# Cross attention of a decoder's first layer: waits for each PSUM bank on its own, and the shifted products of four banks issued obliquely

## The chip, the cores and the metric

The kernel runs on one core of a Trainium2 chip. TensorE (PE) multiplies matrices into eight banks of PSUM, VectorE (DVE) and ScalarE (ACT) read the banks, SyncE (SP) issues transfers. The engines run side by side and meet at semaphores only. The metric is the device time of one launch in microseconds (us), median over runs; lower is better.

## What is computed

The program is a decoder of four layers (attention, cross attention and a feed forward block each) on 16 sequences of 128 tokens of width 256. The change touches layer 0's cross attention alone:

```python
def _L0_xattn_ref(hidden_states, attention_mask, adapter, Wq, Wk, Wv, Wo, gate):
    ...                                   # 32 heads of width 8, rotary tables cos and sin
    scores = jnp.einsum('bhqd,bhkd->bhqk', q, k) * inv_sqrt_d + attention_mask
    w = jax.nn.softmax(scores)            # the row maximum is taken off before exp
    attn_output = jnp.einsum('bhqk,bhkd->bhqd', w, v)
    a_scores = jnp.einsum('bhqd,bhkd->bhqk', q, a_k) * inv_sqrt_d
    a_scores = jnp.tanh(gate) * jax.nn.softmax(a_scores)
    attn_output = attn_output + jnp.einsum('bhqk,bhkd->bhqd', a_scores, a_v)
    return attn_output @ Wo
x = x + _L0_xattn_ref(_layernorm(x), mask, ctx_2048, ...)
```

So each sequence has 64 attention matrices of 128 x 128: 32 of the tokens with themselves (with the mask) and 32 with the context (without it).

## The kernel before

`L0_xattn` is a software pipeline over the 16 sequences (batches). `ring_of_three` runs turns b = -2 to 16, those from 1 to 12 in a loop whose body holds three turns. In turn b, batch b gets its exponentials and its output, batch b+1 ("ahead") its scores and row maxima, batch b+2 ("entering") its projections, and batch b-1 ("behind") its last part. Every engine has its own instruction list in a fixed order, and waits in it on counting semaphores.

`QuadRows` makes the attention of one batch in four rounds i = 0 to 3 (s, c = divmod(i, 2)): rounds 0 and 1 are attention with itself (s = 0), 2 and 3 with the context (s = 1). A round has 16 heads: row group r (four groups of 32 partitions) times slot j (four key sets `kM`, in each of which all heads but one are zero). The four groups write four banks, `work_bank` = banks 2 to 5, called banks 0 to 3 here by their r. The same four banks are used in turn by two kinds of work:

- `scores_tensor` (batch b+1): in rounds 0 and 1 first `mask_tensor`, 16 small products of an identity block with the mask (32 x 32 tiles of the array, 512 columns), then one product per bank (L972, 512 columns). DVE then takes the row maxima of bank after bank (`maxima_vector`, L1037) and counts `top_found` for each.
- `shifts_tensor` (batch b): the mask again in rounds 0 and 1, then per bank four products in the transposed direction (L985, slot j, 128 columns, float32) and four that add the negated maxima (L990, bfloat16). With the last of a bank PE counts `shifted`. ACT takes the exponentials of bank after bank (`exp_scalar`, L1022) and counts `p_ready` for each.

`mix_tensor` (L1003) multiplies the exponentials of a round with v. PE's order in a full turn is: scores(0), a transpose and projections, mix(3) of batch b-1, shifts(0), scores(1), mix(0), shifts(1), projections with wk and wkr (L199), scores(2), mix(1), projection with wo (L208), shifts(2), a transpose of `raw` (L191), projections with wq and wqr, scores(3), mix(2), transposes, shifts(3), projections with wv (L208), a transpose of `raw`. DVE's order is: maxima(0), the layer norm, normalize, maxima(1), split, rotate k (L1329 to L1331), maxima(2), spread keys (L1336), the residual (L888), normalize, rotate q (L1329 to L1331), maxima(3), normalize, split, normalize.

What frees a bank is told by `score_free` and `shift_free`: a score needs the exponentials (`p_ready`) of the round before, a shift needs the maxima (`top_found`) of the scores of the same round. Both take the bank's number r, and the kernel before calls them once a round, with the last bank (`PAIRS` has one group of four and `some[-1]` is 3).

## Time and the profile before

| | |
|---|---|
| median of 3 runs | 4075.38 us (4067.34 to 4081.88) |
| profiled execution, its own time | 4076.79 us |
| its span, first to last instruction | 4075.0 us |
| PE busy over the span | 3285.3 us (81%) |
| DVE / ACT busy | 2605.6 us (64%) / 1758.6 us (43%) |
| granted PE clock, mean | 0.903 |
| L0 cross attention, where the change is | about 140 us to 745 us of the span |
| in 140 to 750 us: PE, DVE, ACT busy | 484.88, 320.30, 243.32 us of 610 |

The whole kernel is a row of such phases with a barrier behind each, so time saved in this one is saved as a whole, and what lies behind it only moves. A row of the timeline gives start, duration over all merged instructions, engine, line, operation and, in brackets, how long the engine had been idle before and what released it. In this program each float32 matmul of the source (transposes apart) is two MATMUL records, a bfloat16 one is one. The ends of matmuls are modelled, so a matmul row ends a little after the next may begin.

### The profile page before, as it was taken

How to read it: one execution, taken by the hardware profiler on the slowest of the kernel's cores; microseconds unless marked ns; L12 is line 12 of the kernel's file. 1: busy time of each engine (PE TensorE's matmuls, PEld its weight loads, DVE VectorE, ACT ScalarE, POOL GpSimd, SP SyncE). 2: the span in 40 equal slices, each digit the busy share in tenths (PEclk: the TensorE clock that was granted, in tenths of full speed). 3: DMA queues.
4: the chain of work that ended last, by engine and by line, in shares of the span. 5: the costliest groups of instructions: out<-in, count | busy, mean ns of one | idle time of the engine just before them, and what ended most of it. 6: DMA issues, size and time to landing. Idle time of an engine off the chain costs nothing. (4 is left out here: it accounts for less than half of the span.)

```text
span 4075.0 us, 78986 instructions
## 1 busy us (share of the span) xinstructions
PE 3285.3 (81%) x29376; PEld 2411.1 (59%) x29376; DVE 2605.6 (64%) x6900; ACT 1758.6 (43%) x3973; POOL 111.7 (3%) x129
## 2 busy tenths in 40 slices
PE   7688887444878889989988995688987799778899
PEld 6455554211655566566656653467876776545788
DVE  6555554688776777767777767777882288475133
ACT  2244433576445666666666663223332244220011
POOL 2000000000000000000000000001100000000000
PEclk9899999655999999999999997897888899888599
DMA  2000000000400000000000002000000000151100
GB/s 91 28 22 22 15 22 7 1 0 5 146 23 2 1 3 1 1 3 1 1 1 3 1 2 89 1 1 19 15 8 0 0 1 0 34 133 30 43 10 10
DMA packets 85655, 81.21 MB, mean 20 GB/s; under 512 B 12528, under 2 KB 78705, under 8 KB 84849
## 3 DMA queue, kind: packets, MB, share of 16 engines
q1 hardware_dynamic: 84288, 77.68, 6.2%
q8 instruction: 128, 2.10, 0.2%
q10 hardware_dynamic: 1200, 1.11, 0.1%
q14 instruction: 39, 0.31, 0.0%
HBM read 76.67 MB, written 2.11 MB: 19 GB/s over the span
## 5 line engine op out<-in xcount | busy, mean ns | idle before, releaser
L3071 PE MATMUL bank<-L1w_w,L1x_xqT 128*128 128x512 f32 x640 | 304.3, 599 | 2.1 <-DVE L1x_xqT L3326 2.1
L3134 PE MATMUL bank<-L1w_wp,L1x_catT 128*128 128x256 f32 x1024 | 244.0, 381 | 12.0 <-ACT L1x_catT L3242 12.0
L1037 DVE TENSOR_REDUCE L0x_top<-bank 128x4 f32<-128x512 f32 x256 | 159.0, 684 | 105.7 <-PE bank L972 104.1
L3332 DVE TENSOR_REDUCE L1x_ssq<-L1x_square 128x4 f32<-128x512 f32 x192 | 131.6, 685 | 148.5 <-ACT L1x_square L3204 144.3
L1022 ACT ACTIVATE L0x_P<-bank,L0x_level 128x512 f32<-128x512 f32 x256 | 154.9, 688 | 160.3 <-PE bank L990 160.3
L3236 ACT ACTIVATE L1x_cat<-bank,L1x_osum 128x128 f32<-128x128 f32 x512 | 146.0, 367 | 170.9 <-DVE L1x_osum L3363 170.9
L3134 PEld LDWEIGHTS bank<-L1w_wp,L1x_catT 128*128 128x128 f32 x1024 | 186.8, 190 | 49.2 <-ACT L1x_catT L3242 15.0
L3119 PE MATMUL bank<-L1x_v,L1x_PT 128*128 128x129 f32 x1024 | 147.2, 286 | 65.3 <-ACT L1x_PT L3231 65.3
L3093 PEld LDWEIGHTS bank<-ident,L1x_hat 128*128 128x128 f32 x768 | 91.3, 143 | 151.7 <-DVE L1x_hat L3342 115.8
L3214 ACT ACTIVATE L1x_hatT<-bank,L1w_affine 128x512 f32<-128x512 f32 x192 | 148.7, 774 | 72.2 <-PE bank L3093 70.1
L3204 ACT ACTIVATE L1x_square<-bank 128x512 f32<-128x512 f32 x192 | 115.5, 602 | 133.9 <-PE bank L3071 133.9
L3071 PEld LDWEIGHTS bank<-L1w_w,L1x_xqT 128*128 128x128 f32 x640 | 114.0, 192 | 97.6 <-issue 91.1
L3119 PEld LDWEIGHTS bank<-L1x_v,L1x_PT 128*128 128x128 f32 x1024 | 124.0, 191 | 80.4 <-ACT L1x_PT L3231 46.0
L3093 PE MATMUL bank<-ident,L1x_hat 128*128 128x128 f32 x768 | 119.0, 282 | 62.9 <-DVE L1x_hat L3342 62.9
L888 DVE TENSOR_TENSOR x_sb<-x_sb,bank 128x256 f32 (+1 forms) x112 | 47.0, 419 | 186.0 <-PE bank L208 184.1
L191 PE MATMUL bank<-ident,xn 128*128 128x128 f32 x320 | 71.8, 309 | 108.2 <-DVE xn L183 40.7
L3225 ACT ACTIVATE L1x_square<-bank,L1x_top 128x128 f32<-128x128 f32 x512 | 150.0, 405 | 0.0
L3101 PE MATMUL bank<-L1x_hatT 128*128 128x128 f32 x1024 | 143.7, 290 | 0.0
L3342 DVE TENSOR_TENSOR L1x_hat<-bank,L1x_inv 128x512 f32<-128x512 f32 x192 | 132.8, 692 | 9.3
L3370 DVE TENSOR_TENSOR L1x_cat<-L1x_cat,L1w_smooth 128x512 f32<-128x512 f32 x128 | 88.7, 693 | 76.3 <-ACT L1x_cat L3236 76.3
L3101 PEld LDWEIGHTS bank<-L1x_hatT 128*128 128x128 f32 x1024 | 134.7, 207 | 0.0
L959 PE MATMUL bank<-L0x_mask,ident 32*32 32x512 f32 x2048 | 76.6, 619 | 65.5 <-ACT L0x_P L1022 30.7
(649 smaller groups left out, 7840.9 us busy)
## 6 DMA issues: line engine op xcount, KB each, us to landing
L0x_mask<-in_maskrows SPq DMA_DIRECT2D x16, 512.0 KB, 3.3
L3w_wg<-in_L_ffn_Wg SPq DMA_DIRECT2D x8, 704.0 KB, 8.7
L3w_wu<-in_L_ffn_Wu SPq DMA_DIRECT2D x8, 704.0 KB, 10.4
L1w_wp<-in_L_xattn_wproj SPq DMA_DIRECT2D x1, 4096.0 KB, 30.0
L3x_ctxT<-in_ctxT SPq DMA_DIRECT2D x32, 128.0 KB, 2.1
L3w_wd<-in_L_ffn_Wd SPq DMA_DIRECT2D x8, 512.0 KB, 9.9
L0x_ctxT<-in_ctxT SPq DMA_DIRECT2D x16, 128.0 KB, 2.9
L1w_w<-in_L_xattn_wq SPq DMA_DIRECT2D x1, 2048.0 KB, 9.6
```

The costliest lines, as they stand in the source:

```text
L1022: act.activation(self.P[:, i % 2, r, :], self.work_bank[r][:, :], ACT.Exp, bias=self.level[:, :]).then_inc(self.p_ready.sem, 1)
L1037: dve.tensor_reduce(self.top[:, s, 16 * c + 4 * r:16 * c + 4 * r + 4], self.work_bank[r][:, :].rearrange("p (h k) -> p h k", h=4), X, ALU.max,
L3071: last = pe.matmul(made_bank[n % 4][:, :], inputs(SOURCE[n], k), w[:, k, 4 * n:4 * n + 4, :], start=(k == 0), stop=(k == C - 1))
L3093: last = pe.transpose(flip_bank[n % 2][:, j * 128:(j + 1) * 128], hat[:, n % 2, j * 128:(j + 1) * 128], kit.ident[:, :])
L3101: last = pe.matmul(made_bank[m % 2][:, j * 128:(j + 1) * 128], hatT[:, q, :], hatT[:, k, :], start=True, stop=True)
L3119: last = pe.matmul(mix_bank[j // 2][:, (j % 2) * (d + 1):(j % 2 + 1) * (d + 1)], PT[:, m % 2, j * 128:(j + 1) * 128], v[:, g, :], start=Tr ...
L3134: last = pe.matmul(y_bank[:, 0:D], catT[:, j, :], wp[:, 4 * m + j, :], start=(m == 0 and j == 0), stop=(m == MG - 1 and j == 3))
L3214: act.activation(hatT[:, 4 * n:4 * n + 4, :], flip_bank[n % 2][:, :], ACT.Identity, scale=affine[:, 0, KIND[n]:KIND[n] + 1], bias=affine[: ...
L3225: last = act.activation(P[:, m % 2, j * 128:(j + 1) * 128], made_bank[m % 2][:, j * 128:(j + 1) * 128], ACT.Exp, bias=top[:, 4 * m + j:4 * ...
L3236: last = act.activation(cat[:, j * d:(j + 1) * d], mix_bank[j // 2][:, (j % 2) * (d + 1):(j % 2) * (d + 1) + d], ACT.Copy, scale=osum[:, j ...
L3332: dve.tensor_reduce(ssq[:, 4 * n:4 * n + 4], square[:, n % 2, :].rearrange("p (h e) -> p h e", h=4), X, ALU.add).then_inc(sum_ready.sem, 1)
L3342: dve.tensor_tensor(hat[:, n % 2, :].rearrange("p (h e) -> p h e", h=4), made_bank[n % 4][:, :].rearrange("p (h e) -> p h e", h=4), part.u ...
```

## The change

Three functions of `QuadRows` are written anew; no product is added or taken away.

- `mask_tensor` makes the mask of one bank: four products, column tiles 0 to 3 (before: 16 products, the bank running fastest).
- `scores_tensor`: in rounds 0 and 1, for each bank in turn its wait and its mask, then the four score products; in rounds 2 and 3, for each bank its wait and its product.
- `shifts_tensor`: the masks likewise; then the 32 products in 11 oblique lines t = 0 to 10, where bank r is at its step t - r (steps 0 to 3 are L985's slots, 4 to 7 L990's). In rounds 2 and 3 bank r's wait stands ahead of its step 0.

```diff
-    def mask_tensor(self, pe, mask, some):
+    def mask_tensor(self, pe, mask, r):
...
+        rows = self.rows_of(r)
         for c in range(4):
-            for r in some:
...
     def scores_tensor(self, pe, n, i, mask, wait_free):
...
-        for some in self.PAIRS:
-            wait_free(i, some[-1])
-            if s == 0:
-                self.mask_tensor(pe, mask, some)
-            for r in some:
-                rows = self.rows_of(r)
-                pe.matmul(self.work_bank[r][:, :], self.qT[n][rows, c, :], self.kM[n][s][rows, c, :, :],
-                          start=(s == 1), stop=True).then_inc(self.scored.sem, 1)
+        if s == 0:
+            for r in range(self.ROWS):
+                wait_free(i, r)
+                self.mask_tensor(pe, mask, r)
+        for r in range(self.ROWS):
+            rows = self.rows_of(r)
+            if s == 1:
+                wait_free(i, r)
+            pe.matmul(self.work_bank[r][:, :], self.qT[n][rows, c, :], self.kM[n][s][rows, c, :, :],
+                      start=(s == 1), stop=True).then_inc(self.scored.sem, 1)
 
     def shifts_tensor(self, pe, n, i, mask_T, wait_free):
...
-            for j in range(self.SLOTS):
-                for r in some:
...
+        def score(r, j):
+            rows = self.rows_of(r)
+            if s == 1 and j == 0:
+                wait_free(i, r)
+            pe.matmul(self.work_bank[r][:, j * 128:(j + 1) * 128], self.kM[n][s][rows, c, j, :], self.qT[n][rows, c, :],
+                      start=(s == 1 and j == 0), stop=False)
+
+        def shift(r, j):
...
+        for t in range(2 * self.SLOTS + self.ROWS - 1):
+            for r in range(self.ROWS):
+                if 0 <= t - r < self.SLOTS:
+                    score(r, t - r)
+                elif self.SLOTS <= t - r < 2 * self.SLOTS:
+                    shift(r, t - r - self.SLOTS)
```

PE's order at shifts(0) of the first full turn, before: the end of the mask, then slot after slot over the four banks (bank2 to bank5 are the four work banks).

```order
L959 MATMUL bank2<-L0x_mask,ident 32x512
L959 MATMUL bank3<-L0x_mask,ident 32x512
L959 MATMUL bank4<-L0x_mask,ident 32x512
L959 MATMUL bank5<-L0x_mask,ident 32x512
L985 MATMUL bank2<-L0x_qT0,L0x_kM00 128x128
L985 MATMUL bank3<-L0x_qT0,L0x_kM00 128x128
L985 MATMUL bank4<-L0x_qT0,L0x_kM00 128x128
L985 MATMUL bank5<-L0x_qT0,L0x_kM00 128x128
```

The same place after: four masks, each with a wait of its own.

```order
L957 MATMUL bank2<-L0x_mask,ident 32x512 [waits L0x_top_found]
L957 MATMUL bank2<-L0x_mask,ident 32x512 x3
L957 MATMUL bank3<-L0x_mask,ident 32x512 [waits L0x_top_found]
L957 MATMUL bank3<-L0x_mask,ident 32x512 x3
L957 MATMUL bank4<-L0x_mask,ident 32x512 [waits L0x_top_found]
L957 MATMUL bank4<-L0x_mask,ident 32x512 x3
L957 MATMUL bank5<-L0x_mask,ident 32x512 [waits L0x_top_found]
L957 MATMUL bank5<-L0x_mask,ident 32x512 x3
```

The single wait ahead of 16 mask products has become four waits; only the last four products stand behind the last bank's. PE's order at shifts(3) (no mask), after; before, one wait stood ahead of all 32 products, which went slot by slot as above.

```order
L987 MATMUL bank2<-L0x_qT0,L0x_kM01 128x128 [waits L0x_top_found]
L987 MATMUL bank2<-L0x_qT0,L0x_kM01 128x128
L987 MATMUL bank3<-L0x_qT0,L0x_kM01 128x128 [waits L0x_top_found]
L987 MATMUL bank2<-L0x_qT0,L0x_kM01 128x128
L987 MATMUL bank3<-L0x_qT0,L0x_kM01 128x128
L987 MATMUL bank4<-L0x_qT0,L0x_kM01 128x128 [waits L0x_top_found]
L987 MATMUL bank2<-L0x_qT0,L0x_kM01 128x128
L987 MATMUL bank3<-L0x_qT0,L0x_kM01 128x128
L987 MATMUL bank4<-L0x_qT0,L0x_kM01 128x128
L987 MATMUL bank5<-L0x_qT0,L0x_kM01 128x128 [waits L0x_top_found]
L992 MATMUL bank2<-L0x_topT,L0x_select 128x128
L987 MATMUL bank3<-L0x_qT0,L0x_kM01 128x128
```

Nine products of the first three banks now stand ahead of the last bank's wait, and each L992 product (L990 before) of the first bank stands between L987 products of others.

## Rows read from the trace of the kernel before

**Rows 1.** The page's groups: count, busy us, mean ns, idle us before and its releasers.

```profile
L1037 DVE TENSOR_REDUCE L0x_top<-bank 128x4 f32<-128x512 f32 x256 | 159.0, 684 | 105.7 <-PE bank L972 104.1
L1022 ACT ACTIVATE L0x_P<-bank,L0x_level 128x512 f32<-128x512 f32 x256 | 154.9, 688 | 160.3 <-PE bank L990 160.3
L959 PE MATMUL bank<-L0x_mask,ident 32*32 32x512 f32 x2048 | 76.6, 619 | 65.5 <-ACT L0x_P L1022 30.7
```

**Rows 2.** Timeline, from exp(0) to exp(1) of one full turn.

```profile
354.88 2.42 ACT L1022 ACTIVATE L0x_P<-bank,L0x_level 128x512 f32<-128x512 f32 x4 [2.22 <-PE bank L990]
...
357.44 1.15 PE L959 MATMUL bank<-L0x_mask,ident 32*32 32x512 f32 x32 [1.88 <-ACT L0x_P L1022]
...
362.32 1.15 PE L959 MATMUL bank<-L0x_mask,ident 32*32 32x512 f32 x32 [1.27 <-DVE L0x_top L1037]
...
363.40 0.98 PEld L985 LDWEIGHTS bank<-L0x_qT,L0x_kM 32*128 32x128 f32 x32 [0.84 <-issue]
...
364.29 0.34 PEld L990 LDWEIGHTS bank<-L0x_topT,L0x_select 32*128 32x128 bf16 x16
...
364.81 2.42 ACT L1022 ACTIVATE L0x_P<-bank,L0x_level 128x512 f32<-128x512 f32 x4 [3.21 <-PE bank L990]
```

**Rows 3.** The same timeline, from exp(1) to exp(3).

```profile
365.72 1.06 PE L199 MATMUL bank<-xnT,L0x_wkr 128*128 128x128 f32 x8
...
367.29 1.14 PE L972 MATMUL bank<-L0x_kM,L0x_qT 32*128 32x512 f32 x8 [0.51 <-ACT L0x_P L1022]
367.74 0.42 DVE L1331 TENSOR_TENSOR L0x_kT<-L0x_kT,L0x_part 128x256 f32<-128x256 f32 x1
...
368.44 2.48 DVE L1037 TENSOR_REDUCE L0x_top<-bank 128x4 f32<-128x512 f32 x4 [0.28 <-PE bank L972]
...
369.37 1.13 PE L208 MATMUL bank<-L0x_wo,L0x_oT 128*128 128x256 f32 x4
...
370.99 1.17 PE L985 MATMUL bank<-L0x_qT,L0x_kM 32*128 32x128 f32 x32 [0.49 <-DVE L0x_top L1037]
...
372.40 2.42 ACT L1022 ACTIVATE L0x_P<-bank,L0x_level 128x512 f32<-128x512 f32 x4 [2.31 <-PE bank L990]
372.51 0.42 PEld L191 LDWEIGHTS bank<-ident,L0x_raw 128*128 128x128 f32 x4 [0.31 <-DVE x_sb L888]
...
375.98 0.42 DVE L1331 TENSOR_TENSOR L0x_qT<-L0x_qT,L0x_part 128x256 f32<-128x256 f32 x1
376.53 2.48 DVE L1037 TENSOR_REDUCE L0x_top<-bank 128x4 f32<-128x512 f32 x4
...
379.07 1.17 PE L985 MATMUL bank<-L0x_qT,L0x_kM 32*128 32x128 f32 x32 [1.37 <-DVE L0x_top L1037]
```

**Rows 4.** The same timeline, from exp(3) to exp(0) of the next turn.

```profile
380.48 2.42 ACT L1022 ACTIVATE L0x_P<-bank,L0x_level 128x512 f32<-128x512 f32 x4 [2.52 <-PE bank L990]
...
382.23 0.60 PE L191 MATMUL bank<-ident,L0x_raw 128*128 128x128 f32 x4
...
383.15 1.15 PE L959 MATMUL bank<-L0x_mask,ident 32*32 32x512 f32 x32 [0.33 <-ACT L0x_P L1022]
...
390.52 2.42 ACT L1022 ACTIVATE L0x_P<-bank,L0x_level 128x512 f32<-128x512 f32 x4 [2.22 <-PE bank L990]
```

**Rows 5.** Timeline at a turn that ends the loop body: PE around the jump.

```profile
311.96 1.15 PE L959 MATMUL bank<-L0x_mask,ident 32*32 32x512 f32 x32 [2.65 <-issue]
```

**Rows 6.** PE's timeline in 326.70 to 327.15: the first part of a mask.

```profile
326.77 0.72 PE L959 MATMUL bank<-L0x_mask,ident 32*32 32x512 f32 x16 [1.27 <-DVE L0x_top L1037]
```

**Rows 7.** PE's timeline in 328.84 to 328.90: from L985 to L990.

```profile
328.63 0.40 PE L985 MATMUL bank<-L0x_qT,L0x_kM 32*128 32x128 f32 x8
328.85 0.23 PE L990 MATMUL bank<-L0x_topT,L0x_select 32*128 32x128 bf16 x4
```

**Rows 8.** Busy time and granted clock (after the engines) of two turns.

```profile
432.00:467.50 35.50, 29.25 (x572) 19.63 (x556) 19.66 (x49) 15.15 (x32) 0.00 (x0) 1.00 0.07 21
467.50:504.00 36.50, 30.71 (x572) 20.40 (x556) 19.65 (x49) 15.00 (x31) 0.00 (x0) 0.95 0.06 20
```

More of the change, by code:

```diff
@@ L903 @@
     ROWS, SLOTS, WIDE, ROUNDS, H, d = 4, 4, 32, 4, 32, 8
-    PAIRS = ((0, 1, 2, 3),)
     SETS = 3
@@ L951, in rows_of @@
         return slice(32 * r, 32 * r + 32)
-    def mask_tensor(self, pe, mask, some):
+    def mask_tensor(self, pe, mask, r):
         pe.sem_inc(self.masking, 1)
+        rows = self.rows_of(r)
         for c in range(4):
-            for r in some:
-                rows = self.rows_of(r)
-                pe.matmul(self.work_bank[r][32 * c:32 * c + 32, :], self.kit.ident[rows, rows],
-                          mask[rows, c, :].unsqueeze(1).to_broadcast([32, 4, 128]), start=True, stop=False,
-                          tile_position=(32 * r, 32 * c))
+            pe.matmul(self.work_bank[r][32 * c:32 * c + 32, :], self.kit.ident[rows, rows],
+                      mask[rows, c, :].unsqueeze(1).to_broadcast([32, 4, 128]), start=True, stop=False,
+                      tile_position=(32 * r, 32 * c))
@@ new lines, in shifts_tensor @@
+        if s == 0:
+            for r in range(self.ROWS):
+                wait_free(i, r)
+                self.mask_tensor(pe, mask_T, r)
+        def score(r, j):
+            rows = self.rows_of(r)
+            if s == 1 and j == 0:
+                wait_free(i, r)
+            pe.matmul(self.work_bank[r][:, j * 128:(j + 1) * 128], self.kM[n][s][rows, c, j, :], self.qT[n][rows, c, :],
+                      start=(s == 1 and j == 0), stop=False)
+        def shift(r, j):
+            rows = self.rows_of(r)
+            last = pe.matmul(self.work_bank[r][:, j * 128:(j + 1) * 128], self.select[rows, j:j + 1].to_broadcast([32, 128]),
+                             self.topT[rows, i, :], start=False, stop=(j == self.SLOTS - 1))
+            if j == self.SLOTS - 1:
+                last.then_inc(self.shifted.sem, 1)
@@ L995, in mix_tensor @@
+        for t in range(2 * self.SLOTS + self.ROWS - 1):
+            for r in range(self.ROWS):
+                if 0 <= t - r < self.SLOTS:
+                    score(r, t - r)
+                elif self.SLOTS <= t - r < 2 * self.SLOTS:
+                    shift(r, t - r - self.SLOTS)
     def mix_tensor(self, pe, b, n, i):
```

15 lines of the change are left out of this document (removed).

## The prediction

> **What bounds the kernel now.** The page says only that the two readers of the four banks are idle half of the phase: DVE waits 104.1 us for scores and ACT 160.3 us for shifts [rows 1]. So I read the timeline of one full turn, from exp(0) at 354.88 to the next at 390.52, 35.64 us [rows 2, 4]. It is a relay: ACT's four exponentials (2.42 us), PE's scores (1.14), DVE's four maxima (2.48), PE's shifts, ACT again. In rounds 0 and 1 the relay has nothing else in it: the mask starts 0.14 us behind exp(0)'s end, the next mask behind the maxima, exp(1) at 364.81 [rows 2]. In round 2 the maxima wait until 368.44, though DVE was done with rotating k at 368.16 [rows 3]. In round 3 the row of the maxima at 376.53 has no bracket: DVE came from other work and set the start itself. After exp(3), which ends at 382.90, PE had been idle only 0.33 us ahead of the mask at 383.15 [rows 4]: it had transposed until 382.83.
>
> **How the array issues.** Whether the oblique order costs anything hangs on this. Of a mask's 32 records 16 start within 0.38 us and are under way together [rows 6], and all 32 take 1.15 us [rows 2]. In the program the two halves of one product stand next to each other, so at least one product per tile starts while an earlier one's second half still waits. I take it that each row group works through its own instructions, and that only semaphore waits and a change of tiling hold all of them. The change of tiling does: after each mask the row of L985's loads shows 0.84 us without any load [rows 2], the time in which the mask's second halves run out.
>
> **The change part by part**, against this turn. Spacing inside a chain of four: maxima (2.48 - 0.68) / 3 = 0.60 us, exponentials (2.42 - 0.69) / 3 = 0.58 us [rows 1, 2].
>
> *Masks, rounds 0 and 1.* Behind the last bank's wait stand 4 products, not 16. The first halves of 16 begin within 0.72 - 0.62 = 0.10 us [rows 6], where 0.62 is one record's mean [rows 1], so 12 fewer save about 0.08 us. The scores cannot start before the last mask is out, so the three banks masked early gain nothing more. Three of the four masks in a turn are waited for (scores(1), shifts(0), shifts(1)): **-0.25 us**. Bounds: 0 and 3 x 0.10 = 0.30. In scores(0) all four banks are free, and nothing is saved.
>
> *Oblique products, rounds 0 and 1.* All banks are ready together. With rows of their own each bank takes what it took, 1.41 us from L985's first load to exp(1) [rows 2]. **0**; the bound above is the first rival.
>
> *scores(2).* PE leaves wkr at about 366.71 (its row ends, modelled, at 366.78). By then banks 0 and 1 are free (exp(1) at 364.81 + 0.69 + 0.58), bank 2 at that moment, bank 3 as before at 367.29. Bank 0 is scored at 366.71 + 1.14 = 367.85, before DVE's rotation ends at 368.16. DVE starts at about 368.29 (0.13 us between a rotation and its maxima, as from 376.40 to 376.53) and not at 368.44: **-0.15 us** for the maxima and for what hangs on them. Bounds: 0 and 0.28, all its idle time [rows 3]. The cover for the rest of the 1.74 us by which bank 0 could be earlier is that rotation.
>
> *shifts(2).* PE leaves L208 at about 370.43, when maxima 0 to 2 are done. Banks 0 to 2 start there instead of at 370.99, and bank 0 is read 1.42 us later, at 371.85: exp(2) begins 0.55 us earlier. But behind it PE waits for the residual (the bracket at 372.51), which DVE makes after the maxima, and then projects; scores(3) follows without a wait. So only the 0.15 us goes on, to rotate q, to maxima(3) and to PE's last part [rows 3].
>
> *shifts(3).* PE idles here for 1.37 us [rows 3] and can use it: bank 0 has made its scores when the last wait falls, and only its four L990 steps follow it: about 0.5 us to exp(3) in place of 1.41. With the 0.15, exp(3) starts and ends about 1 us earlier, at 381.9.
>
> *The end of the turn.* Now the exponentials no longer hold scores(0), PE does. Its transposes end at 382.83, the next tiling can begin at about 382.76, less 0.15, and 0.03 from load to product: 382.64, against 383.15: **-0.51 us**, of which 0.36 is the new part. The slack ahead of this mask differs by a tenth between turns; between the ends 0.15 and 0.51 I take -0.46. Late next is PE's own chain of projections.
>
> Sum for a turn: 0.25 + 0.46 = **0.71 us**, 2% of it. There are 14 turns with all stages. Three of them end in the loop's jump, where PE stands idle 2.65 us for nothing that the profile names [rows 5]; there exp(3) is no limit, only 0.15 + 0.25 is to be had, and three more waits of about 0.1 us each (the 0.14 from exp to mask is two steps) pass before the last mask, since nothing is queued: about 0.1 us remains. Turn 14, without projections, gains more, since DVE's rotation covers nothing there: I estimate 1.5 us from the same steps. Total: 11 x 0.71 + 3 x 0.1 + 1.5 = 9.6, with the first turns' masks **10 us**.
>
> The profiled execution took 4076.79 us, so its sum is 4067. That is 1.4 us above the median of the runs; against the median it is **4065 us**. 0.3% of the median, about what a measurement of this kernel can tell from no change, is 12.2 us, so the forecast lies just inside.
>
> **What the clock adds.** Turns like the one read run at a granted clock of 1.00. A few fell for a short time to the lower level: the window from 467.5 has 0.95, and PE is busy 30.71 us with the 572 records that took 29.25 in the window before, 1.5 us more [rows 8]. Where the falls lie changes with a turn's length, so I add 4 us to either side, and no shift. Own range: 4055 to 4074.
>
> **Rivals.**
>
> *The array issues in the order written.* Then a line of the oblique order lasts as long as its slowest member. From rows 2 an L985 step is (364.29 - 363.40) / 4 = 0.22 us, an L990 step at most 0.34 / 4 = 0.09; I take 0.06, since 0.34 includes the last load's own length. Bank 0's last step stands in line 7, behind seven lines with L985 in them: 7 x 0.22 = 1.54, against 4 x 0.22 + 3 x 0.06 = 1.06: exp 0.48 us later in rounds 0 and 1, and PE is held 0.66 us longer. Rounds 2 and 3 gain 0.18 from the early start. Per turn +0.96 - 0.25 - 0.18 = +0.5 us, over 14 turns +7: 4082, range 4075 to 4090. Against it speaks rows 6. The Trainium skill speaks for it: "TensorE: Matmul & The Clock Gate", under "The mechanism", says that matmuls start and end strictly in program order. By that rule the 16 starts in rows 6 could not be, and the sum would be this rival's 4082.
>
> *The waits cost what they give.* Twelve more waits a turn for banks; if those that find their bank ready are not hidden behind queued products, at 0.1 us each in four rounds, the 0.71 us is used up: 4070 to 4083, likeliest 4077. Against: PE's register and semaphore work seems to run ahead of the array, since no gap stands between L985 and L990.
>
> *Changing between float32 and bfloat16 empties the array.* This one ends slower. Lines 4 to 6 hold both types, six changes a round that one change does today. If each cost 0.2 us (the 0.10 of a load left bare and as much to drain), a turn would gain 4 x 1.2 - 0.71 = 4.1 us, 14 turns 57: 4133. It decides from 0.07 us a change on: 14 x 24 x 0.07 = 23, which is over 10 + 12.2. Against: L990 products run beside L985 products at 328.85 [rows 7], so both types are in the array at once.
>
> *A bank's scores start when its own mask is out*, without the rest. Then DVE starts about 0.85 us earlier in the three waited masks: 14 x 2.5 = 35 on top, 4030. Against: the 0.84 us behind every mask is the full second half of the last one.
>
> **How the numbers follow.** Forecast 0.60; program order 0.18; waits 0.10; types 0.06; own mask 0.06. The range that holds 8 in 10 takes the forecast's own range, program order's and the waits': **4053 to 4087**. Faster by over 0.3% (below 4063.2): 0.6 x 0.42 + 0.06 = 0.31. Slower by over 0.3% (above 4087.6): 0.06 and a third of program order, 0.12. The same: 0.57.
>
> **What would show it.** After, L987 and L992 (the new numbers of L985 and L990) in rounds 0 and 1 should again take 1.41 us from the first load to exp; 1.9 would be program order, over 2.5 the change of types. exp(3) should start about 0.5 us behind the last maximum, not 1.4. The maxima of rounds 0 and 1 should come in one piece 1.1 us behind the last mask; if they start well before, the fourth rival holds. A full turn should take 34.9 us. DVE's idle time ahead of maxima(2) should be under 0.1 us. The forecast falls if scores(0) waits for something other than PE: then the 0.36 is lost, and 5 us is left.

## The result: slower by a third of a percent, where a quarter of a percent faster was forecast

| | before | after |
|---|---|---|
| median of 10 runs each, measured together | 4082.64 us (4067.34 to 4089.56) | 4092.11 us (4076.18 to 4100.11) |
| ratio to before, 95% interval | | 1.0033 (1.0021 to 1.0045) |
| span of the profiled execution | 4075.0 us | 4094.4 us |
| layer 0's cross attention in it | 613.8 us | 633.8 us |
| an ordinary turn at a granted clock of 1.00 | 35.54 us | 36.16 us |
| the three turns that end in the loop's jump | 37.97, 37.97, 38.07 us | 42.88, 42.48, 41.46 us |

The ratio times 4082 us is 13 us of loss (the two medians alone differ by 9.5), and the interval excludes both the forecast (4065) and no change. In the profiled execution all of the difference lies in this phase; the others differ by 2 us at most, with both signs. A turn is counted here from exp(0) to the next exp(0), and numbered by its batch.

The line numbers of after are 9 higher than before from the mix on (L1022 is L1031, L1037 is L1046); L959, L985, L990 are L957, L987, L992. The groups of the page of after, as in [rows 1]:

```profile
L1031 ACT ACTIVATE L0x_P<-bank,L0x_level 128x512 f32<-128x512 f32 x256 | 155.1, 688 | 169.0 <-PE bank L992 169.0
L1046 DVE TENSOR_REDUCE L0x_top<-bank 128x4 f32<-128x512 f32 x256 | 159.0, 683 | 100.6 <-PE bank L972 97.5
L957 PE MATMUL bank<-L0x_mask,ident 32*32 32x512 f32 x2048 | 137.4, 608 | 6.9 <-issue 6.4
```

The work itself takes the same time. DVE waits 6.6 us less for scores than in [rows 1], so the waits for each bank give something. ACT waits 8.7 us more for shifts: that side lost more. The masks' busy time nearly doubled only because products waiting in rows spread out over the wait; their idle time went from 65.5 to 6.9.

The timeline of after, weight loads and exponentials of one ordinary turn, answering [rows 2, 4]:

```profile
354.62 0.37 PEld L957 LDWEIGHTS bank<-L0x_mask,ident 32*32 32x32 f32 x24 [0.17 <-issue]
...
355.14 0.18 PEld L957 LDWEIGHTS bank<-L0x_mask,ident 32*32 32x32 f32 x8 [0.15 <-issue]
...
356.16 0.31 PEld L972 LDWEIGHTS bank<-L0x_kM,L0x_qT 32*128 32x128 f32 x8 [0.84 <-issue]
...
360.96 1.07 PEld L987 LDWEIGHTS bank<-L0x_qT,L0x_kM 32*128 32x128 f32 x24 [0.84 <-issue]
...
362.73 2.42 ACT L1031 ACTIVATE L0x_P<-bank,L0x_level 128x512 f32<-128x512 f32 x4 [2.50 <-PE bank L992]
```

From L987's first load to exp(0) it is 1.77 us now (360.96 to 362.73), where [rows 2] had 1.41. The prediction named 1.41 as the mark of its own case and 1.9 as that of program order; the truth lies at three quarters of the way. And scores(0)'s mask, which starts right behind PE's transposes (0.17 us idle), takes 1.54 us to the scores' load; in the kernel before it was 1.11:

```profile
383.12 0.27 PEld L959 LDWEIGHTS bank<-L0x_mask,ident 32*32 32x32 f32 x32 [0.54 <-issue]
384.23 0.31 PEld L972 LDWEIGHTS bank<-L0x_kM,L0x_qT 32*128 32x128 f32 x8 [0.84 <-issue]
```

Only one turn of three has the 1.54; in the others of after it is 1.27, the turns with the jump apart.

The stretches with the loop's jump, over which the prediction had passed with 0.1 us a turn, are the larger part: 12.8 us of the phase's 20. The same timeline of after, weight loads only:

```profile
313.35 0.95 PEld L957 LDWEIGHTS bank<-L0x_mask,ident 32*32 32x32 f32 x29 [1.78 <-issue]
315.84 0.18 PEld L957 LDWEIGHTS bank<-L0x_mask,ident 32*32 32x32 f32 x3 [1.54 <-issue]
317.68 0.52 PEld L972 LDWEIGHTS bank<-L0x_kM,L0x_qT 32*128 32x128 f32 x8 [1.66 <-issue]
```

After 29 of 32 loads PE stands still, waiting for nothing that the profile can name. In the kernel before the same stop came later, when scores(0) was already out and DVE at work:

```profile
311.93 0.27 PEld L959 LDWEIGHTS bank<-L0x_mask,ident 32*32 32x32 f32 x32 [2.86 <-issue]
...
313.04 0.31 PEld L972 LDWEIGHTS bank<-L0x_kM,L0x_qT 32*128 32x128 f32 x8 [0.84 <-issue]
...
314.49 0.20 PEld L191 LDWEIGHTS bank<-ident,xn 128*128 128x128 f32 x2 [1.13 <-issue]
```

There the stop costs little: 1.13 us where the same row has 0.76 without it (after, at 357.24). And the trace of the loop's own line in the kernel before (engine, operation, count; shortest, median and longest duration in ns) tells what the jump is:

```profile
L1078 PEldq COMPARE_BRANCH  x4: 83/4336/4520, 306.9 to 638.7; - x4
L1078 ACTq COMPARE_BRANCH  x4: 40/45/58, 309.0 to 640.8; - x4
L1078 DVEq COMPARE_BRANCH  x4: 50/62/80, 310.6 to 642.4; - x4
```

PE's three taken branches last over 4 us (3.3 to 3.7 in after), those of ACT and DVE 0.04 to 0.08; in the trace PE's loop body has 3453 instructions, ACT's 161. In both traces the stop ends 3.0 to 3.1 us behind the first instruction that follows the branch: 314.49 behind 311.43 before, 315.84 behind 312.85 after. Counted from that instruction, PE has issued 87 instructions when it stops in the kernel before and 69 in the kernel after, at each of the three jumps. The difference is 18, and 18 is what the turns written out ahead of the loop have grown by, all of it in one line: `mask_tensor` begins with `pe.sem_inc(self.masking, 1)`, for which nothing in the kernel waits. Before it ran once for the four banks, now it runs once for each. The line of the increment in the turns ahead of the loop, before and then after (L955 is L954 now; both from the view of this source line, windows 144 to 198.5 and 142 to 199.7):

```profile
L955 PEldq EVENT_SEMAPHORE  x6: 51/51/3532, 144.4 to 180.6; - x6
L954 PEldq EVENT_SEMAPHORE  x24: 51/51/1762, 142.8 to 181.6; - x24
```

So the stop stands at the same place of PE's code in both kernels. Behind the jump three more increments and three more instructions for the waits (ALU_OP) stand among the masks, and so the place now lies inside them. Between the branch and the stop both traces have one transfer of instructions (queue 8, "instruction", 0.02 MB; 312.1 us before, 313.5 after), so I read the stop as code that has not yet arrived. The Trainium skill, "Runtime: NRT & Kernel Launch", "Instruction fetch mechanics", has this as a rule: PE's instruction memory holds 2048 instructions and is filled in blocks of 256, and a taken branch to a target outside the current window of two blocks has to wait for a fetch. The long branches agree with it; the sizes and where the blocks begin show in no run here, and the second stop shows in the traces alone.

What comes with the stop costs more than the stop itself. The stretch from exp(3) to exp(0) with the first jump, before and then after (length, busy time of PE, PEld, DVE, ACT and POOL, then the granted clock):

```profile
306.97:319.33 12.36, 9.40 (x175) 5.97 (x176) 3.94 (x10) 3.91 (x8) 0.00 (x0) 1.00 0.02 4
309.27:326.57 17.30, 15.09 (x178) 8.81 (x174) 4.21 (x11) 3.92 (x9) 0.00 (x0) 0.80 0.02 4
```

The clock fell to its lower level 0.1 to 1.2 us behind the end of each of the three stops, for 6.8, 6.8 and 3.4 us. From the scores' first load to exp(0) these stretches took 8.89, 9.38 and 8.18 us, where after_2020 below took 6.57 at a granted clock of 1.00: 6.7 of the 12.8 us. In before_plus_18, which has the stop ahead of the scores, the clock fell at all three jumps, too, while PE stood in it; in the kernel before and the six kernels named 2020 it fell at 4 of 21. The fall goes with a stop that PE has to sit out, but three of those 4 are in masks_2020, which has no second stop, so it is not tied to it.

### The profile page after: what moved, and what is told of

Its sections match the earlier page's. It is cut to its first block and busy times, and to the rows that moved or that the text cites. A ratio compares the mean times of both kernels' runs of the same rounds, so it can differ in the third digit from the quotient of the medians.

```text
span 4094.4 us, 79273 instructions
## 1 busy us (share of the span) xinstructions
PE 3406.7 (83%) x29375; PEld 2491.7 (61%) x29376; DVE 2602.8 (64%) x6900; ACT 1760.6 (43%) x3973; POOL 111.8 (3%) x129
## 3 DMA queue, kind: packets, MB, share of 16 engines
q10 hardware_dynamic: 1200, 1.11, 0.1%
## 5 line engine op out<-in xcount | busy, mean ns | idle before, releaser
L1031 ACT ACTIVATE L0x_P<-bank,L0x_level 128x512 f32<-128x512 f32 x256 | 155.1, 688 | 169.0 <-PE bank L992 169.0
L1046 DVE TENSOR_REDUCE L0x_top<-bank 128x4 f32<-128x512 f32 x256 | 159.0, 683 | 100.6 <-PE bank L972 97.5
L3080 PEld LDWEIGHTS bank<-L1w_w,L1x_xqT 128*128 128x128 f32 x640 | 114.0, 192 | 97.6 <-issue 90.9
L957 PE MATMUL bank<-L0x_mask,ident 32*32 32x512 f32 x2048 | 137.4, 608 | 6.9 <-issue 6.4
L987 PEld LDWEIGHTS bank<-L0x_qT,L0x_kM 32*128 32x128 f32 x2048 | 111.0, 188 | 38.3 <-issue 31.7
```

The lines of the kernel that those rows point to most:

```text
L957: pe.matmul(self.work_bank[r][32 * c:32 * c + 32, :], self.kit.ident[rows, rows], mask[rows, c, :].unsqueeze(1).to_broadcast([32, 4, 128]) ...
L1031: act.activation(self.P[:, i % 2, r, :], self.work_bank[r][:, :], ACT.Exp, bias=self.level[:, :]).then_inc(self.p_ready.sem, 1)
L1046: dve.tensor_reduce(self.top[:, s, 16 * c + 4 * r:16 * c + 4 * r + 4], self.work_bank[r][:, :].rearrange("p (h k) -> p h k", h=4), X, ALU.max,
L3080: last = pe.matmul(made_bank[n % 4][:, :], inputs(SOURCE[n], k), w[:, k, 4 * n:4 * n + 4, :], start=(k == 0), stop=(k == C - 1))
```

## The experiments

The theory: (1) the array takes products nearly in the order written, so the oblique order costs in every round; (2) the three long turns are a matter of where the code stands; (3) the waits for each bank gain about what was predicted. Rivals: the waits themselves are the loss, behind the jump or everywhere. "2020" in a label means that the loop's code starts 14 instructions behind the stop's place. It is brought there by semaphore increments that nobody waits for, and these cost 10 to 13 us at the phase's start (its first product comes at 140 to 143 us instead of 130), so times of such kernels are compared among themselves.

| kernel | median us | ratio (95%) | exp 0-1 | 1-2 | 2-3 | 3-0 | turn |
|---|---|---|---|---|---|---|---|
| before | 4081 | 1 | 9.94 | 7.59 | 8.08 | 9.94 | 35.55 |
| after | 4092 | 1.0033 (1.0021 to 1.0045) | 10.10 | 7.40 | 8.08 | 10.59 | 36.17 |
| before_plus_18 | 4095.61 | 1.0034 (1.0021 to 1.0046) | 9.93 | 7.59 | 8.09 | 9.93 | 35.55 |
| before_2020 | 4090.51 | 1.0025 (1.0013 to 1.0037) | 9.94 | 7.58 | 8.08 | 9.94 | 35.54 |
| after_2020 | 4088.52 | 1.0020 (1.0008 to 1.0031) | 10.10 | 7.40 | 8.08 | 10.49 | 36.07 |
| oblique_2020 | 4112.49 | 1.0076 (1.0059 to 1.0093) | 10.29 | 7.97 | 8.43 | 10.28 | 36.97 |
| slots_2020 | 4075.35 | 0.9980 (0.9971 to 0.9990) | 9.76 | 7.37 | 8.08 | 9.97 | 35.18 |
| masks_2020 | 4079.72 | 0.9999 (0.9990 to 1.0008) | 9.76 | 7.58 | 8.09 | 9.94 | 35.37 |
| starts_first_2020 | 4101.81 | 1.0049 (1.0032 to 1.0067) | 10.13 | 7.78 | 8.19 | 10.12 | 36.22 |
| before_unrolled | 4071.13 | 0.9980 (0.9971 to 0.9990) | 9.94 | 7.65 | 8.02 | 9.99 | 35.60 |
| lag_unrolled | 4067.72 | 0.9962 (0.9949 to 0.9975) | 9.75 | 7.66 | 7.86 | 10.30 | 35.57 |
| after_unrolled | 4067.55 | 0.9966 (0.9954 to 0.9979) | 10.11 | 7.39 | 8.09 | 10.28 | 35.87 |
| slots_unrolled | 4053.11 | 0.9930 (0.9916 to 0.9945) | 9.75 | 7.37 | 8.08 | 9.77 | 34.97 |
| slots_unrolled_one | 4064.02 | 0.9961 (0.9947 to 0.9975) | 9.75 | 7.37 | 8.08 | 10.31 | 35.51 |

The columns after the ratio are the starts of the exponentials in one turn of each trace at full clock, with no jump in it. Each ratio is against the runs of before made with that kernel; the first line's time is the median of one of these sets.

**The place of the code.** To the kernel before, this alone was added:

```diff
+            for _ in range(18):
+                pe.sem_inc(at.masking, 1)
             ring_of_three(pe, turn)
```

> The kernel before, with 18 semaphore increments on PE ahead of layer 0's cross attention; nothing waits for them. In the kernel after, PE's loop code in this phase starts 18 instructions later than before, and right behind each jump back of the loop it stands still in the middle of the masks. Theory of the code's place: what counts is how far behind the jump's target the instruction stands at which PE stops for lack of code. With 18 instructions more ahead of it, 18 fewer fit in, the stop falls at the end of the masks or in the four scores, and the three turns that end in a jump take 1.5 to 4 us more than 37.97: the phase 5 to 12 us longer, ordinary turns 35.6 as before. Theory that the new order of the work alone makes the loss: turns with a jump stay at 38.0, and the time is that of the kernel before within 0.1%.

Its turns with a jump took 41.76, 41.46 and 43.15 us, its ordinary ones 35.55, and its time is that of the kernel after, though not one product or wait was changed. The time missed the expected 5 to 12 us upwards (14 us), and much of it is clock: 72.1 us at the lower level in the phase, against 40.3 before. The increments themselves delay nothing here: the phase's first product comes at 130.3 us instead of 130.4. The timeline of this kernel behind the first jump:

```profile
316.06 0.32 PEld L959 LDWEIGHTS bank<-L0x_mask,ident 32*32 32x32 f32 x32 [2.65 <-issue]
318.76 0.52 PEld L972 LDWEIGHTS bank<-L0x_kM,L0x_qT 32*128 32x128 f32 x8 [2.38 <-issue]
```

All masks are out, and the four products of the scores are not yet there: the stop has moved to exactly between them, 69 instructions behind the branch as in the kernel after, 2.38 us instead of 0.84.

The other way, code moved past the place, with 102 increments in the kernel before and 84 in the kernel after:

> The kernel before, with 102 semaphore increments on PE ahead of layer 0's cross attention, so that the loop's code starts some 10 instructions behind the place at which PE stops after a jump. Theory of the code's place: the stop, the row with 1.13 us of idle time at the first transposes behind each jump, moves 256 instructions back to where PE waits anyway or has run far enough, and the turns with a jump take 37 to 38 us (37.97 before): 0 to 3 us less in all. Ordinary turns 35.6. The added increments cost at most 102 x 0.1 = 10 us, once, if the phase's start does not hide them; they stand where PE waits for its weights. Theory without place: no change in any turn.

> The kernel after, with 84 semaphore increments on PE ahead of the phase, so that its loop starts at the same place as in the run before this one. Theory of the code's place: the turns with a jump fall from 42.9, 42.5 and 41.5 to about 38.5, the phase gets 10 to 13 us shorter than in the kernel after, and what is left is 11 ordinary turns at 36.17 against 35.6, 6 to 8 us over the kernel before: ratio about 1.0015 to 1.002 in place of 1.0033. Theory that the per-bank waits themselves hold PE behind a jump: the turns with a jump stay over 41 us and the ratio stays 1.0033.

```profile
324.34 0.91 PEld L957 LDWEIGHTS bank<-L0x_mask,ident 32*32 32x32 f32 x32 [1.69 <-issue]
326.09 0.31 PEld L972 LDWEIGHTS bank<-L0x_kM,L0x_qT 32*128 32x128 f32 x8 [0.84 <-issue]
```

In after_2020 (rows above) the stop is gone; its turns with a jump took 37.90, 39.47 and 37.87 us in place of 42.88, 42.48 and 41.46, 11.6 us less in all, while the branch still lasts up to 3.6 us. The added increments eat most of it in the total. In before_2020 those turns took 38.22, 36.80 and 38.60, but two of them had a fall of the clock in exp 0-1. The stretch with the jump itself took 11.40, 11.19 and 11.45 us in place of 12.37, 12.36 and 12.46, 3.1 us less in all, the upper end of the expected 0 to 3: the branches are shorter at this place (3.3 to 3.6 us instead of 4.2 to 4.5). Theory (2) stands: the same waits, placed elsewhere, do not stop behind a jump. They still are not free there: the masks' loads take 0.91 us behind the jump (row above) where before_2020 has 0.27. And with the loop at the same place the whole change is no slower than the kernel before, 4088.52 us against 4090.51, though its ordinary turns are 0.3 to 0.5 us longer and it has 18 increments fewer.

**The oblique order alone**, in the kernel before, behind its one wait:

```diff
-            for j in range(self.SLOTS):
-                for r in some:
...
+            for t in range(2 * self.SLOTS + self.ROWS - 1):
+                for r in some:
+                    if 0 <= t - r < self.SLOTS:
+                        score(r, t - r)
+                    elif self.SLOTS <= t - r < 2 * self.SLOTS:
+                        shift(r, t - r - self.SLOTS)
```

> The kernel before with the oblique order of the shifted products alone: one wait for all four banks as before, masks as before; the loop's code starts at the same place as in the two runs before this one. Theory that the array issues almost in program order: exp follows L985's first load by 1.77 us instead of 1.41 in rounds 0 and 1, and in rounds 2 and 3, too, since nothing starts early; a turn takes 0.3 x 4 less what other work hides in rounds 2 and 3: 36.3 to 36.8 instead of 35.6, the whole 10 to 17 us over the kernel before. Theory that each row group goes by itself: 1.41 us in all rounds and 35.6 us a turn.

Each of the four stretches grew by 0.34 to 0.39 us and the turn by 1.43, to 36.97 where at most 36.8 was expected; the time is 22 us over before_2020, above the expected 10 to 17. The slowest change tested, with no wait added. Why, is seen in the loads. Timelines of PE's loads in one round, a window that ends within 0.1 us of the first load and one that ends 0.3 us behind it (both begin at the same load, the last number ahead of the bracket counts); before_2020, then oblique_2020:

```profile
444.13 0.20 PEld L985 LDWEIGHTS bank<-L0x_qT,L0x_kM 32*128 32x128 f32 x4 [0.84 <-issue]
...
444.13 0.42 PEld L985 LDWEIGHTS bank<-L0x_qT,L0x_kM 32*128 32x128 f32 x12 [0.84 <-issue]
```

```profile
440.75 0.20 PEld L984 LDWEIGHTS bank<-L0x_qT,L0x_kM 32*128 32x128 f32 x2 [1.61 <-DVE L0x_top L1043]
...
440.75 0.41 PEld L984 LDWEIGHTS bank<-L0x_qT,L0x_kM 32*128 32x128 f32 x5 [1.61 <-DVE L0x_top L1043]
```

In slot order four loads start within 0.02 us, one per row group, and twelve by 0.24. Obliquely it is two within 0.02 and five by 0.22; the other groups follow at 0.33 us (bank 2) and 0.56 us (bank 3). A group's own loads are 0.11 us apart, which tells the banks apart. This is neither the order written nor free groups: bank 1's first load, at 0.01 us, passes the second half of bank 0's first product and both halves of its second one, which come at 0.11 to 0.33. But bank 2's, which stands behind three products of bank 0 and two of bank 1, has to wait. The matmuls themselves do the same. In oblique_2020, in a window that ends 0.1 us behind their first start, two are under way, and no third starts before 0.21 us:

```profile
440.75 0.39 PE L984 MATMUL bank<-L0x_qT,L0x_kM 32*128 32x128 f32 x2 [1.37 <-DVE L0x_top L1043]
```

So I formed a finer theory, that a row group takes in about two float32 products, and that one more for a full group holds up all that is written behind it. The test turns the banks of each line around, so that bank 2's first product has two of bank 0's ahead of it and not three:

```diff
             for t in range(2 * self.SLOTS + self.ROWS - 1):
-                for r in some:
+                for r in reversed(some):
```

> The kernel of oblique_2020 with the banks of each line in the opposite order: bank 3's product first, bank 0's last. In oblique_2020 the first loads of banks 0 to 3 came at 0, 0.01, 0.33 and 0.56 us, in the kernel before at 0, 0.01, 0.01 and 0.02. Theory that a row group takes in about two float32 products and that whatever stands in the program behind a product whose group is full has to wait, whatever its own group is: bank 2's first product now has only one product of bank 1 and two of bank 0 ahead of it and starts at 0.02; bank 3's has bank 0's third ahead of it and starts at 0.3. exp then starts 0.1 to 0.3 us earlier than in oblique_2020 (1.77 us behind the first load) and a turn takes 36.0 to 36.8 instead of 36.97. Rival, that the array issues strictly in the order written or that lines go in lockstep: banks 2 and 3 start at 0.33 and 0.56 or later, and a turn takes 36.97 or more.

```profile
450.21 0.20 PEld L984 LDWEIGHTS bank<-L0x_qT,L0x_kM 32*128 32x128 f32 x3 [0.84 <-issue]
...
450.21 0.41 PEld L984 LDWEIGHTS bank<-L0x_qT,L0x_kM 32*128 32x128 f32 x8 [0.84 <-issue]
```

(The second window ends at 0.29.) Three loads within 0.02 us and the fourth group's at 0.33, as expected, and a turn of 36.22 where strict order would have kept 36.97. Its time (4102) is 11 us below oblique_2020's. The finer theory passed this one test; whether the limit is counted in products, passes or instructions stays open, and only float32 products were tried.

**The waits without the oblique order**, and the masks alone:

```diff
-        for t in range(2 * self.SLOTS + self.ROWS - 1):
...
+        for step in (score, shift):
+            for j in range(self.SLOTS):
+                for r in range(self.ROWS):
+                    step(r, j)
```

> The kernel after with the shifted products back in slot order (all four banks' step j, then all four banks' step j + 1), every per-bank wait kept; the loop's code at the same place as in the other runs of that name. Theory that the oblique order costs 0.36 us in each of four rounds: exp follows the last mask's load by the old time again in rounds 0 and 1, a turn without a jump falls from 36.0 (after_2020) to about 35.3 to 35.5, a little below the 35.54 of the kernel before, since the early masks of three waited rounds remain (-0.2); round 3 loses its early start. Time 5 to 10 us below after_2020. Theory that the waits are the dearer part: a turn stays over 35.8.

masks_2020 is slots_2020 with one wait for the products again (shown for the shifts; the scores of rounds 2 and 3 have the same edit):

```diff
-            if s == 1 and j == 0:
-                wait_free(i, r)
+            if s == 1 and j == 0 and r == 0:
+                wait_free(i, self.ROWS - 1)
```

> The kernel before with the masks written bank by bank behind a wait each, the products in slot order behind one wait as before; the loop's code at the same place. Theory: shifts(0), shifts(1) and scores(1) gain about 0.08 us each as the prediction said, scores(0), where all banks are free, loses 0.43 (four waits stand between the masks with nothing to hide them), so a turn takes 35.54 + 0.43 - 0.25 = 35.7. Rival, that scores(0)'s loss is hidden by other work or was another thing: 35.3.

From after_2020 to slots_2020 a turn lost 0.89 us and the time 13 us: 0.34 in exp 0-1, nearly nothing in the stretches with rounds 2 and 3, and 0.52 at the end. Both are more than expected (a turn of 35.3 to 35.5, 5 to 10 us), and the loss of 0.36 in each of four rounds did not show; I take it that where the banks start early, this pays for the oblique order. masks_2020, which has a wait of its own per bank only in the masks, keeps 0.18 of the gain; the waits in rounds 2 and 3 are worth the other 0.21 (exp 1-2). My expectation for masks_2020, a loss of 0.43 at scores(0), fell: 35.37 against the rival's 35.3. Its turns with a jump took 41.11, 38.79 and 41.42 us, which looks like the stop again but is the clock. Its timeline behind the first jump:

```profile
321.99 2.12 PE L957 MATMUL bank<-L0x_mask,ident 32*32 32x512 f32 x32 [1.52 <-issue]
324.04 2.09 PE L972 MATMUL bank<-L0x_kM,L0x_qT 32*128 32x512 f32 x8
```

The scores take 2.09 us in place of 1.14 [rows 3], at the lower of the two levels (a granted clock of 0.77 from exp(3) to exp(0)), after PE had stood idle at the jump.

**No loop.** PE's code of the phase written out:

```diff
-            ring_of_three(pe, turn)
+            for b in range(-2, B + 1):
+                turn(b, b % 3, b)
```

> The kernel before with PE's loop of the phase written out: 16 turns of code and no jump, constants in place of registers in the waits. Theory that PE's jump makes the three long turns (37.97 against 35.55) and nothing else does: all turns take 35.5, 7 us less in all, and the instructions' place no longer matters. Rival, that straight code is fetched no better, and PE stops at each 256 instructions, or that the other engines' own jumps then end last: the three turns stay over 37 us, or all turns get longer.

In lag_unrolled the products of shifts(3) go like this, with bank 3 two steps behind, and bank 2's wait ahead of bank 0's first step:

```diff
+        early = 2 if i == self.ROUNDS - 1 else 0
+        for t in range(2 * self.SLOTS + early):
+            for r in range(self.ROWS):
+                k = t - (early if r == self.ROWS - 1 else 0)
```

> The run before this one with four changes that the runs so far speak for: masks behind per-bank waits in scores(1), shifts(0) and shifts(1) but one wait in scores(0); slot order everywhere; in shifts(3) the banks 0 to 2 make two steps behind bank 2's wait, ahead of bank 3's, which follows two steps behind them. Theory: -0.2 us a turn from the masks, and exp(3) 0.4 us earlier, of which the 0.3 us that PE has been idle ahead of scores(0) is the most that can be had: a turn of 35.1 to 35.3 against 35.5, 3 to 6 us below before_unrolled. Rival, that what stands between the groups costs what it gives: no difference.

> The kernel of slots_2020 (per-bank waits in all rounds, products in slot order) without its 84 increments and with PE's loop written out. From slots_2020: its ordinary turns took 35.18 and 35.00, its three turns with a jump 37.1, and its increments cost some 10 us at the phase's start. Theory that these add up: turns of 35.1 throughout, and about 10 + 3 x 2 = 16 us below slots_2020: ratio to the kernel before 0.995, 4060 us. Rival, that written-out code has its own price (before_unrolled's turns took 35.60, not 35.54, and lag_unrolled's 35.58 although it has the early masks): turns of 35.4 to 35.6, ratio 0.996.

> The kernel after with PE's loop written out, so that it has no jump. Theory that the loss of the kernel after is the oblique order (0.89 us a turn by slots_2020 against after_2020) and the code's place behind the jumps, and nothing else: turns of 36.0 throughout, some 12 us above slots_unrolled, and near before_unrolled + 5 us: ratio 0.999 to 1.000. Rival, that the three long turns were something other than the jump: they stay over 38.

Written out, no kernel has a long turn: 35.60 in before_unrolled where three had 37.97, and 35.87 or 35.88 in twelve turns of after_unrolled. Straight code of 16 turns shows no such stop. The loops of ACT and DVE stayed and cost nothing. With the jump gone, the undisturbed turn reads: before_unrolled 35.60, waits without the oblique order 34.97 (-0.63), all of the change 35.87 (+0.27).

The times tell more. after_unrolled was expected at a ratio of 0.999 to 1.000 and came out at 0.9966: 4067.55 us against 4071.13 of before_unrolled, whose interval overlaps. So without a jump the whole change is not slower, in spite of the 0.27 us a turn. In the profiled executions the turns 1 to 13 take 467.1 us together in before_unrolled and 466.7 in after_unrolled, since the clock fell in five of the one and in none of the other; one profile of each does not show that this is the rule. The oblique order costs the 14 us from slots_unrolled to after_unrolled.

slots_unrolled took 34.97 us in nearly all its turns, less than slots_2020 (35.18 and 35.00), so the rival's price for written-out code did not show. It is **4053.11 us, ratio 0.9930 (0.9916 to 0.9945)**, below the expected 4060 and faster than both kernels of the case. Its page has DVE waiting 80.5 us for scores and ACT 156.9 for shifts:

```profile
L1029 ACT ACTIVATE L0x_P<-bank,L0x_level 128x512 f32<-128x512 f32 x256 | 154.9, 688 | 156.9 <-PE bank L992 156.9
L1044 DVE TENSOR_REDUCE L0x_top<-bank 128x4 f32<-128x512 f32 x256 | 159.1, 683 | 83.7 <-PE bank L972 80.5
```

lag_unrolled missed its 35.1 to 35.3. exp 2-3 gained 0.16 us (7.86), but one wait at scores(0) stands in it, and the turn's end took 10.30. What that wait costs, the last run tells, slots_unrolled with

```diff
+            if i == 0:
+                wait_free(i, self.ROWS - 1)
             for r in range(self.ROWS):
-                wait_free(i, r)
+                if i > 0:
+                    wait_free(i, r)
                 self.mask_tensor(pe, mask, r)
```

> slots_unrolled with one wait ahead of scores(0)'s masks instead of four, since all four banks are free there. Theory that four waits between masks that nobody has to wait for cost 0.43 us at the end of each turn (the kernel after took 1.54 us from the first mask's load to the scores' in place of 1.11): 0.3 to 0.4 us a turn below slots_unrolled, 5 us in all. Rival, that other work hides them, as masks_2020 has it (35.37 in place of the 35.7 that they would give): the same within 0.1%.

Both theories were wrong: it lost 0.54 us a turn, all at the end. slots_unrolled there, and then slots_unrolled_one:

```profile
340.52 2.42 ACT L1029 ACTIVATE L0x_P<-bank,L0x_level 128x512 f32<-128x512 f32 x4 [2.47 <-PE bank L992]
...
342.07 0.57 PEld L191 LDWEIGHTS bank<-ident,L0x_raw 128*128 128x128 f32 x4
...
342.82 0.43 PEld L957 LDWEIGHTS bank<-L0x_mask,ident 32*32 32x32 f32 x32 [0.17 <-issue]
...
344.09 0.31 PEld L972 LDWEIGHTS bank<-L0x_kM,L0x_qT 32*128 32x128 f32 x8 [0.84 <-issue]
```

```profile
343.78 2.42 ACT L1032 ACTIVATE L0x_P<-bank,L0x_level 128x512 f32<-128x512 f32 x4 [2.47 <-PE bank L995]
...
346.43 0.63 PEld L957 LDWEIGHTS bank<-L0x_mask,ident 32*32 32x32 f32 x32 [0.51 <-issue]
...
347.89 0.31 PEld L975 LDWEIGHTS bank<-L0x_kM,L0x_qT 32*128 32x128 f32 x8 [0.84 <-issue]
```

From exp(3) to the mask it is 2.30 us in the first and 2.65 in the second. In the first the mask of bank 0 follows PE's own transposes while ACT still reads bank 3 (until 342.94); in the second all four masks wait for that end (346.20). The four banks are not all free there, as the prediction and I had taken them to be. From mask to scores it is 1.27 and 1.46: the loads' row is 0.43 and 0.63 long in place of the 0.27 of a mask in one piece. What stands between the pieces here is the increment of `masking` (and the waits, in the first); no run left the increments out, so their share of this price is not shown.

## Why the prediction was wrong, point by point

Two steps failed. That the array issues row group by row group, with the oblique order at 0, was wrong: the order costs 0.36 us in rounds 0 and 1 and 14 us of the time, more than the forecast gain of 10. And the three turns with a jump, at 0.1 us gained, lost 12.8 us in the profiled execution. The first ate the gain; only the second made it a loss, since with the loop at another place, or written out, the whole change is not slower.

- **How the array issues.** From 16 masks starting together it concluded that each row group works through its own list. But a 32 x 32 tile has only one product in a mask, so by the finer theory none fills up, and the row could not show a limit. The chance of 0.18 for the rival was too small, although its sizes were nearly right: +0.48 foretold and +0.36 found for rounds 0 and 1, PE held 0.66 foretold and 0.54 found (the loads run over 1.34 us instead of 0.80), +0.5 a turn foretold and +0.27 (written out) to +0.6 (in the loop) found. The Trainium skill's rule in "TensorE: Matmul & The Clock Gate", "The mechanism", that matmuls start strictly in program order, gives the sign but not the trace: in oblique_2020 bank 1's first matmul starts 0.01 us behind bank 0's first and 0.20 ahead of bank 0's next, and three passes of bank 0 stand ahead of it in the program. That this rival's range of 4075 to 4090 holds the measured ratio (4089 against the median it started from) is in part luck, since the jump is in it.
- **The oblique order in rounds 0 and 1: 0.** It was 0.36 us a round; that is 0.72 of the 0.90 between slots_unrolled and after_unrolled, and the rest is PE being later at the turn's end (the mask of scores(0) starts 2.47 us behind exp(3) instead of 2.30).
- **Masks: -0.25.** Right in kind and nearly in size: 0.18 for the two of them in exp 0-1 (0.09 each, 0.08 foretold).
- **scores(2) and shifts(2): -0.15, bounds 0 and 0.28.** Measured -0.21 (7.58 to 7.37), and -0.28 written out. As foretold, DVE's rotation covers the rest: the maxima of round 2 have no idle bracket in after.
- **shifts(3): exp(3) 0.5 us behind the last maximum.** It was 1.26 (before 1.47). The early start of banks 0 to 2 is paid for by the oblique order behind it, I take it; that was not tested apart. And exp 2-3 stayed 8.08, since the maxima of round 3 came 0.22 us later (4.35 us behind exp(2) instead of 4.13). lag_unrolled, which starts banks 0 to 2 early without the oblique order, had exp 2-3 at 7.86, and kept it: its turn's end took 10.30, that of slots_unrolled_one, with the same single wait at scores(0), 10.31.
- **The end of the turn: -0.46.** The condition came true, but another way than foretold: in after and in slots_unrolled, PE's transposes and not ACT set scores(0) (0.17 us idle ahead of the mask's load), although exp 2-3 had not become shorter. Bank 0's mask waits for bank 0 alone, which the prediction had put at nothing ("In scores(0) all four banks are free"); with one wait the turn is 0.54 us longer (slots_unrolled_one). The size was not right: with slot order the stretch fell from 9.99 to 9.77, of which 0.09 is shifts(0)'s mask. The mask starts 0.34 us earlier behind exp(3) (2.30 instead of 2.64), but in four pieces it takes 1.27 us to the scores instead of 1.11, a price that the sum set at nothing. In the loop it was 1.54 in one turn of three of the kernel after.
- **The sum without the oblique order** was 0.71 us a turn, measured 0.63 written out. That the two are so near is in part luck: -0.19, -0.28, +0.06 and -0.22 in the four stretches, where the forecast had most of it at the end. The forecast's mechanisms were right in the main for the kernel slots_unrolled, and wrong for the kernel that was built. The time gained there, 18 us against before_unrolled, is more than these turns make; the phase in the profiled execution is 12.4 us shorter, with 16 us less at the lower clock level.
- **Turn 14: 1.5 us gained.** At a granted clock of 1.00 it took 30.65 us in before_plus_18, 30.36 in after_2020 and 28.96 in slots_unrolled_one. So the estimate holds for slot order (-1.7) and not for the kernel after (-0.3).
- **Three turns with a jump: 0.1 us gained.** They lost 12.8 us together in the profiled execution (126.8 against 114.0), over half of it at the lower clock level behind the stop. The prediction had the row of 2.65 us idle "for nothing that the profile names" [rows 5] and did not ask what it was. That is the second step that failed, and no rival held it. before_plus_18 shows that the place of the code, with the clock that goes with it, suffices for the measured ratio. The 18 instructions that moved the code are increments of `masking`, of which neither the section on the change nor the prediction speaks.
- **The clock: 4 us to either side.** This was too small for the profiled execution. The phase of after had 63.8 us at the lower level, that of before 40.3. Of the 63.8, 17.0 lie behind the three stops and 10.2 in turn 15, where exp(0) to exp(3) took 20.6 us instead of 15.8. Falls come in ordinary turns, too, in five of the ten ones from 1 to 13 before and in two after. What sets them there is not shown.
- **The other two rivals.** Neither shows: L987's first load to exp(0) is 1.77 us and not over 2.5, and the maxima start 1.16 us behind the scores' load as before (356.16 to 357.32; 313.04 to 314.20 in the kernel before), with no head start for a bank whose own mask is out.
- **The loop's remainder.** A turn of after is 36.17 in the loop and 35.87 written out. In after the second turn of the body loses it in exp 0-1 (10.42) and the first at scores(0); at place 2020 one of the two is gone (35.89). I read it as code place and register work of the waits, but that was not tested apart.

## What to carry to other kernels

Before adding instructions to a loop whose body is long (here 3453 on one engine), look at the duration of the branch and at the first idle row marked "issue" behind it: what is added ahead of the loop, too, moves the place where the engine stops. Count what a helper issues besides its products: here an increment that nobody waits for was multiplied by four. Writing the loop out removed the stop altogether, and made 0.2% for the unchanged kernel. And on products in several row groups: write them so that every group gets one before any group gets its third, and read the starts of single loads in a stretch where groups have several products each, not one.

## What was not expected of the hardware

- A taken branch of PE to a far target lasts 3.3 to 4.5 us (ACT's and DVE's 0.04 to 0.08), and about 3 us behind its end a second stop can follow, at a fixed place of the code (87 instructions behind the branch in the kernel before, 69 with 18 more ahead of the loop); 18 increments ahead of a loop cost 14 us in 4081, with the clock's falls behind the stop.
- A row group held up products of other groups: with two float32 products of bank 0 ahead, bank 2's first load came at 0.02 us, with three at 0.33.
- A mask's 32 loads take 0.27 us in one piece and 0.43 to 0.71 us cut in four by semaphore instructions, even where nothing is waited for; 0.91 right behind a jump.
- 102 semaphore increments in a row cost PE 13 us (143.5 against 130.4 us for the first product of the phase), 0.13 us each.
